# Mixture of experts in a gated cross-attention block: from all tokens through all experts to rows in expert slots

## The reference

```python
logits = einsum('btd,ed->bte', layernorm(x), Wr)
top_vals, top_idx = top_k(logits, 2);  w = softmax(top_vals)
C = int(Tt * 2 / 8 * 1.5) + 1                      # 97 slots of an expert in a batch
pos = how many (token, choice) pairs before this one chose the same expert
dst = expert * C + pos, dropped where pos >= C
expert_out = einsum('becd,edf->becf', rows_in_slots, We)
out = w[0] * expert_out[dst0] + w[1] * expert_out[dst1]
x = x + tanh(g_ffn) * out
```

## Time and profile before

| | us |
|---|---|
| median of 3 runs (1390.58 to 1393.33) | 1391.57 |
| span of the profiled execution | 1388.5 |
| outside of the span, against the median | 3.1 |
| TensorE busy | 1364.6 |
| VectorE busy | 1046.5 |
| ScalarE busy | 913.9 |
| GpSimd busy | 775.2 |

### The profile page before, as it was taken

One profiled execution on the slowest core, in us unless ns is written; L12 is line 12 of the kernel. 1 busy time (PEld: TensorE's weight loads), 2 busy tenths in 40 slices (PEclk: granted clock), 3 DMA queues, 4 the chain that ended last, 5 costly groups with the idle time before them and its releaser, 6 DMA issues. The chain is left out here.

```text
span 1388.5 us, 26883 instructions
## 1 busy us (share of the span) xinstructions
PE 1364.6 (98%) x8116; PEld 1137.0 (82%) x8116; DVE 1046.5 (75%) x3057; ACT 913.9 (66%) x2600; POOL 775.2 (56%) x947
## 2 busy tenths in 40 slices
PE   7899999999999999999999999999999999999998
PEld 6688888888888888888888888888888888888876
DVE  6877877777877777877778777778777788777763
ACT  6776666775666766667766667666677666676652
POOL 4355555656555656555555566565555555555644
PEclk9999999999999999999999999999999999999999
DMA  5001101011111011110111010111110110101000
GB/s 164 30 18 46 45 28 45 18 45 45 37 37 45 18 46 45 32 42 25 38 45 45 29 45 18 45 45 36 38 39 24 45 45 31 43 18 46 25 16 23
DMA packets 70289, 53.72 MB, mean 39 GB/s; under 512 B 45888, under 2 KB 53504, under 8 KB 70144
## 3 DMA queue, kind: packets, MB, share of 16 engines
q1 hardware_dynamic: 70144, 52.00, 12.1%
HBM read 25.11 MB, written 16.78 MB: 30 GB/s over the span
## 5 line engine op out<-in xcount | busy, mean ns | idle before, releaser
L332 PE MATMUL bkM<-we,x2T 128*128 128x512 f32 x3072 | 791.7, 400 | 0.8 <-DVE acc_v L1067 0.7
L332 PEld LDWEIGHTS bkM<-we,x2T 128*128 128x128 f32 x3072 | 553.6, 188 | 127.6 <-ACT a_out L684 8.4
L684 ACT ACTIVATE a_out<-bkM,gate 128x256 f32<-128x256 f32 x512 | 217.0, 482 | 161.1 <-PE bkM L332 159.9
L1067 DVE SCALAR_TENSOR_TENSOR acc_v<-bkM,gate,acc_v 128x256 f32<-128x256 f32 x384 | 184.8, 481 | 106.2 <-PE bkM L332 91.3
L498 POOL TENSOR_TENSOR a_sum<-a_sum,a_out 128x256 f32<-128x256 f32 x256 | 188.9, 738 | 56.8 <-ACT a_out L684 20.5
L485 POOL TENSOR_TENSOR probs<-probs,p_inv 128x308 f32<-128x308 f32 x128 | 89.8, 702 | 211.6 <-DVE p_inv L960 211.6
L453 POOL TENSOR_TENSOR rstd<-ve,minus_half 128x4 f32<-128x4 f32 x64 | 65.2, 1019 | 145.6 <-DVE ve L872 145.4
L453 POOL TENSOR_TENSOR q_r<-q_ve,minus_half 128x8 f32<-128x8 f32 x64 | 105.0, 1642 | 48.6 <-DVE q_ve L945 48.6
L590 ACT ACTIVATE xn<-x_sb,shift,rstd 128x256 f32<-128x256 f32 x128 | 66.5, 590 | 92.4 <-DVE shift L881 92.4
L453 POOL TENSOR_TENSOR k_r<-k_ve,minus_half 77x8 f32<-77x8 f32 x32 | 52.4, 1637 | 126.9 <-DVE k_ve L921 126.9
L503 POOL TENSOR_TENSOR y<-a_sum,acc_v 128x256 f32<-128x256 f32 x128 | 94.4, 738 | 17.3 <-issue 0.4
(11 more groups left out here) (178 smaller groups left out, 2714.7 us busy)
## 6 DMA issues: line engine op xcount, KB each, us to landing
x_sb<-in_x SPq DMA_DIRECT2D x32, 512.0 KB, 3.7
out<-y SPq DMA_DIRECT2D x64, 256.0 KB, 2.0
ctx_sb<-in_ctx SPq DMA_DIRECT2D x32, 154.0 KB
vf<-v_nat SPq DMA_DIRECT2D x64, 77.0 KB
stage<-in_L_ffn_We SPq DMA_DIRECT2D x2, 1024.0 KB, 7.1
vf<-v_nat SPq DMA_DIRECT2D x32, 52.0 KB
vf<-v_nat SPq DMA_DIRECT2D x32, 51.0 KB
vf<-v_nat SPq DMA_DIRECT2D x32, 26.0 KB
```

The source lines that it names most:

```text
L332: mm = nc.tensor.matmul(out, l, r, start=(i == 0), stop=(i == len(terms) - 1))
L684: ins = nc.scalar.activation(a_out[:, t % 2, (e // 4) * 2 + i], bkM[1][:, i * D:(i + 1) * D], ACT.Copy, scale=gate[:, m.parity, t, e:e + 1])
L1067: nc.vector.scalar_tensor_tensor(out=acc_v[:, t], in0=bkM[0][:, i * D:(i + 1) * D], scalar=gate[:, m.parity, t, e:e + 1], in1=src, op0=ALU ...
```

## The change

Each token's normalised row is now sent by GpSimd with indirect DMAs to two rows of a memory in HBM (`in_rows`, one for each batch of the pair), whose row numbers `idx` say which slot of which expert it has (`scatter`). Row position * 8 + (7 - expert) puts one slot of all 8 experts side by side, so that SP loads 112 slots of all experts as one tile of 112 partitions (`load_rows`). TensorE transposes the slots of two experts (`unit_transpose`), ScalarE and VectorE make hi and lo, and TensorE multiplies the 97 slots of each by that expert's matrix alone (`experts`). ScalarE copies the results, SP stores them to `out_rows`, and GpSimd fetches each token's two rows with indirect DMAs (`gather`); VectorE adds them with their weights (`combine`). Tokens past slot 97 meet rows of zeros, which are written once in the fill. There are 8 units of two experts for a pair, in place of 16 chunks. The work of a pair is spread over three rounds: `m` has scatters and units 0 to 5, `c`, the pair before it, has units 6 and 7, the product of unit 5, and the end. There is one round more. The dense experts, the gates for all experts and the sums on three engines go. Attention, routing and their orders stay, but for the slots in which the expert work lies.

```diff
-        SLOTS = T * E // 2
+        SLOTS = 16
+        UNITS_OF = E // 2
+
+        CLEARS = 2 * BP * 16
+        STAGE_USED = FRONT_WEIGHTS + KC * (E // 2)
+
+
+        T_AT = {7: (0, 0), 8: (0, 1), 9: (0, 2), 10: (0, 3), 11: (0, 4), 12: (0, 5), 2: (1, 6), 3: (1, 7)}
+        E_AT = {8: (0, 0), 9: (0, 1), 10: (0, 2), 11: (0, 3), 12: (0, 4), 1: (1, 5), 3: (1, 6), 4: (1, 7)}
+
+        def unit_at(table, k, c, m):
+            late, u = table.get(k, (0, None))
+            pair = (m, c)[late]
+            return (pair, u) if u is not None and pair else None
...
-            for n in range(PAIRS):
-                step(pair(n), pair(n + 1), pair(n + 2), pair(n + 3))
+            for n in range(PAIRS + 1):
+                step(pair(n - 1) if n else None, pair(n), pair(n + 1), pair(n + 2), pair(n + 3))
...
+            def load_rows(m, b):
+
...
+                sp.wait_ge(scattered[b].sem, scattered[b].at(m))
...
+                sp.wait_ge(unit_ps.sem, max(unit_ps.at(m, (b + 1) * UNITS_OF - UNITS), 0))
...
+                sp.dma_start(slots_in[0:PAD, b], in_d[b][0:PAD * E].rearrange("(p j) d -> p (j d)", j=E)
+                             ).then_inc(rows_in[b].sem, 16)
+
+            def store_rows(m, b, i):
+
+                sp.wait_ge(expert_out.sem, expert_out.at(m, b * UNITS_OF + (i + 1) * UNITS_OF // 2))
...
+                sp.wait_ge(gathered[b].sem, gathered[b].before(m))
...
+                half = E // 2 * D
+                sp.dma_start(out_d[b][0:PAD * E].rearrange("(p j) d -> p (j d)", j=E)[:, i * half:(i + 1) * half],
+                             slots_out[0:PAD, i]).then_inc(rows_out[b][i].sem, 16)
...
-            def step(m, p, f, ahead):
+            def step(c, m, p, f, ahead):
+                if m:
+                    load_rows(m, 0)
+                if c:
+                    store(c, 0)
+                    store_rows(c, 1, 0)
+                if f:
+                    put_v(f)
+                if m:
+                    load_rows(m, 1)
+                if c:
+                    store_rows(c, 1, 1)
                 if ahead:
                     load(ahead)
-                if f:
-                    put_v(f)
-                store(m, 0)
-                store(m, 1)
+                if c:
+                    store(c, 1)
+                if m:
+                    store_rows(m, 0, 0)
+                    store_rows(m, 0, 1)
...
-            def finish_tile(m, t):
...
-                    nc.gpsimd.tensor_tensor(a, o[:, 0] if i == 1 else a, o[:, i], ALU.add
-                                            ).then_inc(a_summed.sem, 1)
-                pool.wait_ge(v_added.sem, v_added.at(m, 4 * (t + 1)))
-                pool.wait_ge(a_summed.sem, a_summed.at(m, 3 * t + 3))
-                pool.wait_ge(y_out[t // SUB].sem, y_out[t // SUB].before(m))
-                nc.gpsimd.tensor_tensor(y[:, t], a, acc_v[:, t], ALU.add).then_inc(y_done[t].sem, 1)
...
+            def scatter(m, b):
...
+                pool.wait_ge(rows_in[b].sem, rows_in[b].before(m))
...
+                for t in range(b * SUB, (b + 1) * SUB):
+                    for k in range(TOPK):
+                        nc.gpsimd.indirect_dma_start(
+                            out=in_d[b], out_offset=bass.IndirectOffsetOnAxis(ap=idx[:, m.parity, k, t:t + 1], axis=0),
+                            in_=xn2[:, m.parity, t], in_offset=None).then_inc(scattered[b].sem, 16)
...
+            def gather(m, b):
+
+                for i in range(2):
+                    pool.wait_ge(rows_out[b][i].sem, rows_out[b][i].at(m))
...
+                for t in range(b * SUB, (b + 1) * SUB):
+                    pool.wait_ge(y_done[t].sem, y_done[t].before(m))
...
+                    for k in range(TOPK):
+                        nc.gpsimd.indirect_dma_start(
+                            out=fetched[:, k, t], out_offset=None, in_=out_d[b],
+                            in_offset=bass.IndirectOffsetOnAxis(ap=idx[:, m.parity, k, t:t + 1], axis=0)
+                        ).then_inc(gathered[b].sem, 16)
...
+            def round_of(c, m, p, f):
                 if f:
                     ln1(f)
                 if m:
-                    finish_tile(m, 0)
+                    scatter(m, 0)
                 if p:
                     ln2(p)
+                if m:
+                    scatter(m, 1)
                 if f:
                     k_rsqrt(f)
-                if m:
-                    finish_tile(m, 1)
-                if f:
-                    make_xb(f, 0)
                     q_rsqrt(f, 0)
                     q_rsqrt(f, 1)
-                    make_xb(f, 1)
-                    make_xb(f, 3)
-                    make_xb(f, 2)
-                    normalise(f, 0)
-                    normalise(f, 1)
-                    normalise(f, 2)
-                    normalise(f, 3)
+                if c:
+                    gather(c, 1)
+                if f:
+                    for t in (0, 1, 3, 2):
+                        make_xb(f, t)
+                    for t in range(T):
+                        normalise(f, t)
                 if m:
-                    finish_tile(m, 2)
-                    finish_tile(m, 3)
+                    gather(m, 0)
...
+            def unit_hi_part(m, u):
+                act.wait_ge(unit_ps.sem, unit_ps.at(m, u + 1))
+                act.wait_ge(expert_ps.sem, max(expert_ps.at(m, u - 1), 0))
+                copy(slots_T[:, u % 2, 0], bkM[:, 0:KC * 2 * CAP]).then_inc(unit_hi.sem, 1)
...
+            def expert_part(m, u):
+                b, i = divmod(u, UNITS_OF)
+                act.wait_ge(expert_ps.sem, expert_ps.at(m, u + 1))
+                h = i // 2
+                act.wait_ge(rows_out[1 - b][h].sem, rows_out[1 - b][h].at(m) if b else rows_out[1 - b][h].before(m))
+                act.wait_ge(cleared, CLEARS)
+                copy(slots_out[0:CAP, h, i % 2 * 2 * D:(i % 2 + 1) * 2 * D], bkN[0:CAP]).then_inc(expert_out.sem, 1)
...
+                if k != 9:
+                    unit_out(k, c, m)
...
+            def place(p):
...
+                nc.vector.tensor_tensor(placed[:], mask[:].rearrange("p k t e -> p k (t e)"),
+                                        pos_ps.unsqueeze(1).to_broadcast([P, TOPK, T * E]), ALU.mult
+                                        ).then_inc(place_chain.sem, 1)
...
+                nc.vector.tensor_reduce(row[:], placed[:].rearrange("p k (t e) -> p (k t) e", e=E), AX.X, ALU.add
+                                        ).then_inc(place_chain.sem, 1)
...
-                    nc.vector.scalar_tensor_tensor(
-                        out=gate[:, p.parity, b * SUB:(b + 1) * SUB],
-                        in0=pos_ps.rearrange("p (s b e) -> p b s e", s=SUB, b=BP)[:, b], scalar=float(CAP),
-                        in1=g_all[:, b * SUB:(b + 1) * SUB], op0=ALU.is_lt, op1=ALU.mult
-                    ).then_inc(gate_chain.sem, 1)
...
+                    dve.wait_ge(gathered[b].sem, gathered[b].before(p, 2))
+                dve.wait_ge(place_chain.sem, place_chain.at(p, 2))
+                nc.vector.scalar_tensor_tensor(out=idx[:, p.parity].rearrange("p k t -> p (k t)"), in0=row[:],
+                                               scalar=-1.0, in1=first[:].rearrange("p k t -> p (k t)"),
+                                               op0=ALU.add, op1=ALU.add).then_inc(place_chain.sem, 1)
...
+            def combine(c, b):
+
+                w = w_top[:, c.parity]
+                dve.wait_ge(gathered[b].sem, gathered[b].at(c))
+                dve.wait_ge(y_out[b].sem, y_out[b].before(c))
+                for t in range(b * SUB, (b + 1) * SUB):
+                    nc.vector.scalar_tensor_tensor(out=y[:, t], in0=fetched[:, 0, t], scalar=w[:, 0, t:t + 1],
+                                                   in1=x1[:, c.n % X1_BUFS, t], op0=ALU.mult, op1=ALU.add
+                                                   ).then_inc(first_added.sem, 1)
+                for t in range(b * SUB, (b + 1) * SUB):
+                    dve.wait_ge(first_added.sem, first_added.at(c, t + 1))
+                    nc.vector.scalar_tensor_tensor(out=y[:, t], in0=fetched[:, 1, t], scalar=w[:, 1, t:t + 1],
+                                                   in1=y[:, t], op0=ALU.mult, op1=ALU.add).then_inc(y_done[t].sem, 1)
...
+            def slot(k, c, m, p, f):
+
+                if k not in (3, 7, 9):
+                    next_unit(k, c, m)
...
+                if k == 2 and c:
+                    combine(c, 0)
                 if k == 10:
-                    chunk(k, m, p)
+                    if c:
+                        combine(c, 1)
...
-            def moe(m, c):
...
-                lhs = x2T[:, m.parity]
-                product(bkM[c % 2][:], [
-                    ([lhs[:, a, k, t * P:(t + 1) * P] for a in range(2)],
-                     [we[:, a, k, ep * 512:(ep + 1) * 512] for a in range(2)]) for k in range(KC)]).then_inc(moe_ps.sem, 1)
...
+            def unit_transpose(m, u):
```

(25 more changed lines are left out.)

298 lines of the change are left out of this document (140 added, 158 removed).

## The result

The changed kernel takes 1673.94 us (median of 5, 1658.79 to 1676.39) against 1390.62 (1389.38 to 1393.33): a ratio of 1.2012, 95% interval 1.1969 to 1.2055. It is slower, as forecast, but by 283 us where the forecast was 145, and outside the range. The profiled run took 1658.8 with a span of 1656.9 and is the fastest of the five; the median is 15 us above it.

The account below looks back on a forecast made before the run. Before the change, TensorE's matmul throughput was taken as the bound; after it, a chain of waits. Forecast: 3 outside the span + 65 fill + 30 rounds x 46.5 + 74 tail = 1537 us, range 1310 to 1650.

Parts of the forecast that it names:

- the four additions end at t 31.2: VectorE's weighted additions of batch 1, after waiting 1.4 us for gathers, end 31.2 us after the round's GpSimd rstd.
- the term of 74 us: Tail after the full rounds: three rounds that only wait, estimated at 74 us against 54 before.
- break-even of 41.6: Round length in us below which the changed kernel would be faster than the one before.
- rival (4): TensorE saves less than claimed if short products go at the weight load's pace; 6 us more possible; no chance given.
- X: GpSimd's cost to issue one indirect DMA: taken as 1.1 us, with ends 0.87 and 1.64.
- the walk: Step-by-step sum of one round through all engines, counted from GpSimd's rstd: 31.2 + 5.65 + 9.7 = 46.5 us.
- Rival (2): GpSimd becomes the bound through its indirect DMAs, deciding from 1.2 us each; all rounds above 50 us: chance 0.13.
- Slot 10, the rows' chain: After SP's v pieces, slot load and store land in 5.5 us (4.8 to 9.3); gathers 4.4, last landing 2.0.
- Slot 5 to 9: From k_r to the scores: kn ends at 14.6 us after rstd, first row maximum 22.4, unit 3's residue 27.9.
- Slots 10 to 0: After the additions, 5.65 us to the first pT residue, then 9.7 to the next rstd, instead of 10.7.
- Rival (1): Waits overlap and matmuls stay near the bound: round 34 to 41, middle 37.7, total time 1273 us; chance 0.27.
- Rival (3): DMAs are the bound: slot rows add 5.7 MB a round, 18 us of 46, hidden except latencies; small chance.

Follow-up runs that it names:

- k_r first: Changed kernel with GpSimd computing k_r ahead of the last of the eight scatters, not behind it: 1677.61 us, ratio 1.2053.
- early store: Changed kernel with SP storing the last half of a batch's expert rows ahead of the v pieces and the next load: 1604.16 us, ratio 1.155.
- xb first: Changed kernel with GpSimd making the four xb sums before the gathers of batch 1, not behind them: 1640.44 us, ratio 1.1797.
- last kernel of the orders: Changed kernel with store, xb and k_r moved earlier, both batches' additions later, q products together, second k and v product in a gap: 1448.78 us.

## Why the forecast was right in sign and wrong in size

The mechanism, a chain of waits and not busy time, was right; what failed are terms of its sum. In the round it is the step "the four additions end at t 31.2": they end at t 36.1, because both chains into slot 10 were priced too short, that of the rows by 4.0 us and that of the scores by 4.6, and the additions themselves by 1.0. Later slots, 2.0 us too long, hid part of that (49.5 for 46.5 in this round). In the tail it is the term of 74 us, which measured 112. The sign is not luck: the round is above the forecast's break-even of 41.6 even with no dispatch at all (44.0).

- **What TensorE saves.** Right within 2 us. A unit's 12 products take 1.48 (707.61 to 709.09 in TensorE's timeline) for 1.42, its four transposes 0.28 for up to 0.43, and where a round of the same work ran at full clock TensorE was busy for 36.0 us, forecast 34 (eight units' products and transposes come to 14.1 of the 14.4 that were priced, so the 2 us lie elsewhere, and were not traced). Twelve short products do not run at another pace, so rival (4) does not hold.
- **X, an indirect DMA on GpSimd.** Up to the last v residue the walk held, t 11.7 for 12.0. An indirect DMA occupies GpSimd for 0.96 to 0.99 us, within the range from the earlier trace rows, but the next begins 0.30 after its end: 1.25 to 1.29 where the walk took 1.1. The 0.30 is in no row ahead of the prediction. kn ends at t 15.8 for 14.6, and the scatters at 13.4 for 12.1. Of these 1.3 only 0.45 is X. The walk let the second four scatters begin where ln2's rstd begins (7.7) and so left out that operation's own 1.2 us; they begin at 8.5. Rival (2) was to decide from X = 1.2. At 1.27 k_r is indeed behind the scatters, but GpSimd is busy for 28 of 49 us and does not bound the round. By the Trainium skill (DMA: Bandwidth & Descriptors, Anatomy of one DMA), whose small cost of issue would have given a round of 45.1, the gathers would have landed by t 25 and been harmless; the trace does not agree, each holds the engine for 0.96 us.
- **Slot 10, the rows' chain: its landings are the single term that was mis-sized most in the round.** The v pieces end at t 18.6 for 17.4 (6.72 us of issue for 5.25). The load behind them also waits for the landing of the last scatter, which comes 6.35 us after its issue, at 729.57, just behind the pieces' end at 729.40; the walk had no such wait. It fits with the run with k_r first, where the last scatter came later and the waits for gathered rows grew. From the end of the pieces to the first gather the trace has 8.2 us: 0.85 until the store is issued, 6.4 until it has landed (the chain's own row for it), 0.9 until GpSimd goes on. I took 5.5 out of a span of 4.8 to 9.3, near the floor. That choice cost 2.7 us. The gathers take 4.8 for 4.4, and VectorE goes on at 33.3 for 29.3. The early store shows what the chain's lateness is worth on the whole: 1.5 us a round, of which some 0.8 is the lead of this chain over that of the scores and the rest the additions, which then no longer run beside xb.
- **The additions.** Priced as those they replace (1.85 for four), they take 1.76 alone and 2.88 beside xb. The step "priced as those removed" failed: the removed ones read a bank of PSUM (bkM), these read SBUF alone. With xb elsewhere the round is 0.8 shorter. They end at t 36.1 for 31.2. The Trainium skill (GPSIMD Engine Reference, 1. Specifications) says that GpSimd shares its SBUF interfaces with VectorE and contends with VectorE's instructions of two SBUF inputs; the trace agrees: a pair of additions takes 1.57 us beside xb and 0.88 in slot 2 (one takes 610 ns in the mean of the run, and 481 with xb first). This was the passage to weigh before pricing the additions, and I had not.
- **Slot 5 to 9.** Between kn and the first row maximum the walk had 7.8 us and the trace 9.8 (t 15.8 to 25.6). About 1 us of it is the q product at 1.2 GHz, which the forecast named as what would make it wrong and did not price; 0.5 us a round is what filling that gap gave. From the first row maximum to the end of unit 3's residue the walk had 5.5 us and the trace 6.9 (t 25.6 to 32.5): the residue waits 1.47 for ScalarE, whose copy stands behind four exponentials. With the 1.2 us of kn these are the 4.6 us of the scores' chain, which was as late as that of the rows.
- **Slots 10 to 0.** 5.2 for 5.65, and 8.1 for 9.7 (752.19 to 760.33, the next rstd): forecast 2.0 too long, which hid part of the error.
- **The waits, not the busy time.** The forecast's main reason, that the order of the engines and not busy time holds the round, is shown: 44.0 us with no dispatch at all, and 49.2 to 42.9 through orders alone, with every DMA in place. Most of the loss against the kernel before, 5.2 of 7.0 us, goes with the dispatch all the same: its transfers count as links of the chains. Rival (1), overlap to 37.7, has no support in any run. Rival (3) falls too: the DMA engines are busy for 0.47 of a round of 49.2, and for 0.54 of one of 42.9 with the same transfers.
- **The tail: 112 for 74, a third of the miss.** I added landings and products for "three rounds that only wait" and gave a sum whose working the prediction does not show. The chain of the tail has two trips through DRAM in each round, one behind the other: SP's store of y waits for the additions of batch 1 (from 1576.67), and the rows of batch 0, whose last copy on ScalarE ends at 1572.8, stand behind it on SP. That this order sets the length is not shown: with both the additions and that store moved back the tail was 97.0 for 100.8, where 10 us had been expected. The chain that ended last, in order of time (start, us, what):

```profile
1562.85 6.32 DMA out_rows<-slots_out
...
1573.89 2.76 DMA fetched<-out_rows,idx
1576.67 0.88 DVE y L1135 x2
...
1579.50 4.22 DMA out_rows<-slots_out
...
1598.73 5.97 DMA in_rows<-xn,idx
...
1605.35 6.46 DMA out_rows<-slots_out
...
1616.54 2.75 DMA fetched<-out_rows,idx
```

  From one store of the last half to the next are 42.5 us, and there are two such rounds and a half. TensorE works 54 us of the 112, at a granted clock of 0.72. The runs size its parts, which are not a sum: 39 us less without the indirect DMAs, 29 less without SP's copies, 45 less without both; 11 less from the early store.
- **The fill** was 68.3 for 65. The clearing of the memories holds up SP (one of its issues takes 9.43 us, and the six v pieces behind it 16.8), but TensorE does not wait for v in the second pair. What came instead: with two chunks gone the last products of the fill run at the lower clock (granted 0.50 from 63 to 66), 2.90 us where 1.65 was.
- **The range** was closed at 1650, which the forecast's own terms do not give: the landings at 9.3 alone make 1537 + 30 x 3.8 = 1651, and with X = 1.64 (90), the clearing (21) and the tail (10) as well the sum is some 1770 (an estimate from the forecast's own prices). It left out that several links could be at their dear end at once, and gave the tail 10 us either way where it was off by 38.

## What to carry to other kernels

When a bound engine is relieved, walk the chain that takes its place link by link, and where a link's cost has two ends, put it at the dear end in at least one full sum: late links on one chain add up. An edit that shortens one of two chains that end together gives little or nothing by itself, so look for what ends second before pricing it, and judge edits in pairs. Count the drain of a longer pipeline on its own, by the trips that lie one behind the other, not by its work.

## What the runs showed of the hardware

- An indirect DMA of 128 rows of 1 KB holds GpSimd for 0.96 (gather) to 0.99 us (scatter), and 0.30 pass before the next: 512 of them are 500 us of busy time and some 140 of gaps. A scatter lands 3.3 us after its issue (median; 6.35 for the last one of the round shown, which runs beside the v pieces), a gather 2.8.
- VectorE's additions with three SBUF operands take 0.48 us alone or beside indirect DMAs, and 0.66 to 0.79 where GpSimd works on SBUF tiles beside them. GpSimd's xb is slower then too: 785 ns in the mean of the changed kernel, 738 with xb first.
- SP's issue of six v pieces takes, in the median of the rounds, 5.2 us in the kernel before and wherever the indirect DMAs, SP's copies or both are left out, 6.1 in the changed kernel (5.2 to 7.2) and 6.4 with the store of the last half ahead of them (5.2 to 8.3), but 5.25 in the last kernel of the orders, where two stores stand directly ahead of them. So it got longer only where both parts of the dispatch were there, and not in every order; beside which transfers is open.
- The granted clock of the full rounds is 0.93 in the changed kernel and 1.00 in the last kernel of the orders. In the round shown of the one (0.97), TensorE's two longest gaps are 2.73 and 2.23 us (ahead of unit 5 and of kn's transposes), in that of the other 1.50. In the round at 710.83 the clock falls to 1.2 GHz behind the gap of 2.23 us, and filling it kept it at 2.4. Behind the gap of 2.73 us it did not fall in this round (1.00 from 748 to 751); behind one of 3.60 us in the same place of the round before it was 1.2 GHz (0.50 from 697 to 702).
